# CIN tower with gathered embeddings: the first step's shifted x picked by TensorE instead of read back from DRAM

## What is computed

```
e = stack([tbl_f[ids[:, f]] for f in 39])            # (1024, 39, 16), x of the CIN
z   = einsum('bfd,bgd->bfgd', x, h)                  # h = x in layer 0
cur = relu(einsum('bfgd,fgl->bld', z, Wr) + b)       # L = 128; first half is the next h, second half goes out
out = concatenate(directs).sum(-1), then three dense layers with dense_ctx
```

## Time and profile before

| | |
|---|---|
| median of three runs | 1298.85 us |
| profiled execution | 1300.39 us, its span 1298.5 us |
| TensorE (PE) busy | 1229.6 us, 95% of the span |
| VectorE (DVE) busy | 1046.4 us, 81% |
| GpSimd (POOL) busy | 1068.2 us, 82% |
| ScalarE (ACT) busy | 750.6 us, 58% |
| mean granted TensorE clock | 0.996 |
| chain that ended last | PE 87%, POOL 4%, DVE 4%, issue 3% |

### The profile page before, as it was taken

One profiled execution on the slowest core, in us unless ns is written; L12 is line 12 of the kernel. 1 busy time (PEld: TensorE's weight loads), 2 busy tenths in 40 slices (PEclk: granted clock), 3 DMA queues, 4 the chain that ended last, 5 costly groups with the idle time before them and its releaser, 6 DMA issues.

```text
span 1298.5 us, 13246 instructions
## 1 busy us (share of the span) xinstructions
PE 1229.6 (95%) x4084; PEld 745.5 (57%) x4084; DVE 1046.4 (81%) x943; ACT 750.6 (58%) x931; POOL 1068.2 (82%) x627
## 2 busy tenths in 40 slices
PE   0379999999999999999999999999999999999999
PEld 0335555655665656655665556656656566666655
DVE  2069998888888888988888888888888888988941
ACT  1135665656555666556556656566556677777643
POOL 7528899888988898888989798888888778889942
PEclk9989999999999999999999999999999999999999
DMA  9195566655555666655556676545556665556100
GB/s 184 37 216 121 125 142 145 145 119 110 124 117 116 140 145 145 136 115 111 123 114 129 144 145 135 131 103 125 119 119 141 144 142 108 130 118 161 33 0 1
DMA packets 103424, 157.68 MB, mean 121 GB/s; under 512 B 20954, under 2 KB 33131, under 8 KB 103245
## 3 DMA queue, kind: packets, MB, share of 16 engines
q1 hardware_dynamic: 93179, 154.16, 53.5%
q0 software_dynamic: 10176, 2.70, 2.2%
HBM read 152.91 MB, written 6.19 MB: 123 GB/s over the span
## 4 chain that ended last, share of the span: by engine, by line
PE 87%; POOL 4%; DVE 4%; issue 3%; ACT 1%; DMA 1%; SPq 0%; DVEq 0%; ACTq 0%; POOLq 0%
PE curM L858 36%; PE curM L881 11%; PE curM L873 11%; PE curM L874 11%; PE curY L858 10%; POOL emb L305 3%; DVE z L566 2%; PE xk L847 2%; PE h L964 1%; PE curY L881 1%; PE curY L873 1%; PE curY L874 1%; DVE zl L619 1%; POOL zl L316 1%; ACT h L725 1%
## 5 line engine op out<-in xcount | busy, mean ns | idle before, releaser
L316 POOL TENSOR_TENSOR zl<-z,zh 128x1024 fp32r<-128x1024 f32 (+1 forms) x299 | 724.1, 2433 | 118.1 <-ACT zh L698 112.6
L566 DVE TENSOR_TENSOR z<-xr,h 128x1024 f32<-128x1024 f32 x576 | 677.4, 1216 | 154.5 <-PE curM L858 129.1
L698 ACT ACTIVATE zh<-z 128x1024 fp32r<-128x1024 f32 (+1 forms) x376 | 396.4, 1057 | 387.3 <-DVE z L566 243.4
L858 PE MATMUL curM<-z,wf 128*128 128x512 f32 (+2 forms) x1194 | 537.7, 600 | 0.0
L305 POOL DMA_INDIRECT emb<-in_tbl_dram,idx x312 | 337.6, 1082 | 100.1 <-issue 57.5
L873 PE MATMUL curM<-zh,wl 128*128 128x512 f32 (+1 forms) x642 | 340.7, 531 | 4.2 <-ACT zh L698 4.2
L858 PEld LDWEIGHTS curM<-z,wf 128*128 128x128 f32 (+2 forms) x1194 | 208.5, 188 | 195.2 <-issue 171.6
L874 PE MATMUL curM<-zh,wh 128*128 128x512 f32 (+1 forms) x642 | 251.8, 392 | 0.0
L881 PE MATMUL curM<-zl,wh 128*128 128x512 f32 (+1 forms) x642 | 200.7, 394 | 6.1 <-DVE zl L619 3.6
L873 PEld LDWEIGHTS curM<-zh,wl 128*128 128x128 f32 (+1 forms) x642 | 121.7, 190 | 72.7 <-issue 47.4
L725 ACT ACTIVATE h<-curM,bias 32x512 f32<-32x512 f32 (+1 forms) x198 | 127.9, 646 | 57.5 <-DVE z L566 51.1
(11 more groups left out here) (107 smaller groups left out, 436.9 us busy)
## 6 DMA issues: line engine op xcount, KB each, us to landing
xr<-xT SPq DMA_DIRECT2D x384, 192.0 KB
xs<-xT SPq DMA_DIRECT2D x288, 156.0 KB
xq<-xT SPq DMA_DIRECT2D x64, 256.0 KB
emb<-in_tbl_dram,idx POOLq DMA_INDIRECT x312
xs<-xT SPq DMA_DIRECT2D x64, 78.0 KB
xT<-xc SPq DMA_DIRECT2D x32, 78.0 KB
xr<-in_L_rec_W_dram SPq DMA_DIRECT2D x16, 144.0 KB
xT<-xc SPq DMA_DIRECT2D x32, 40.0 KB
```

What stands on the lines that cost most here:

```text
L316: nc.gpsimd.tensor_tensor(zl[0:n, SNUM[r, u] % NL, :], z[0:n, z_slot(r, u), :], zh[0:n, SNUM[r, u] % NH, :], ALU.subtract).then_inc(lo_poo ...
L566: return nc.vector.tensor_tensor(z[:, slot, :].rearrange("p (a n) -> p a n", a=2), x, h, ALU.mult)
L698: nc.scalar.activation(zh[0:n, SNUM[r, u] % NH, :], z[0:n, z_slot(r, u), :], ACT.Copy).then_inc(hi_ready, 1)
L858: mm = nc.tensor.matmul(cur[:, :], wf[rows, full_at(u), a, :], z[rows, z_slot(r, u), a * N:(a + 1) * N], start=start and i == 0, stop=stop ...
```

## The change

For step 0 alone, `xs` no longer comes through DRAM. VectorE lays out, from the identity matrix, a matrix `picks` of 39 x 117 for each of the seven tiles (2 + 21 small copies, ahead of its wait for `dense_turned`). TensorE multiplies `picks` by `xc` of step 0: seven float32 matmuls of 512 columns give the shifted rows in PSUM (h1 twice, curM[0], curM[1]). ScalarE copies them to `xs` in five instructions (`copy_picked`), and `product0` of step 0 waits for `x0_copied` in place of the DMAs.

SyncE loses the 11 DMAs of `load_xs(0, p)`. It now waits for `xT_written[1]` first and reads `xs` of step 1 part by part, with the write of step 2's x ahead of the last part; the waits for the weights and for `xT_written[0]` come after. `copy_xc` of step 2 moves behind the five new copies on ScalarE, and `turn` of step 2 behind the first four picks on TensorE. The matmuls without a reader go from 28 to 40, and stand ahead of the turns: they start once the first 32 gathers have landed. The count of 16 in `kind` gets the name POOL_FROM and keeps its value, and so do EARLY_FIELDS and BETWEEN, so the gathers keep their order.

```diff
+POOL_FROM = 16
-    return "D" if k == "G" and (r < 0 or (r == 0 and u < 16)) else k
+    return "D" if k == "G" and (r < 0 or (r == 0 and u < POOL_FROM)) else k
-WARM = 28
+WARM = 40
+PICKED = (1, 3, 4, 5)
+        wrapped = xr[1][0:F, 20 * L:20 * L + XR]
+        picks = xr[1][0:F, 21 * L:21 * L + T0 * R0].rearrange("p (t m) -> p t m", m=R0)
@@ sync
             write_x(1, 1)
+            sp.wait_ge(xT_written[1], 32)
+            for p in range(4):
+                sp.wait_ge(z_ready, NUM[-3, C_END + p] + 1)
+                load_xs(1, p)
+                if p == 2:
+                    sp.wait_ge(xc_copied, 3)
+                    write_x(2, 0)
             sp.wait_ge(w_hi, HI_OPS)
             sp.wait_ge(w_lo, LO_OPS)
             sp.wait_ge(w_full, FULL_OPS)
             sp.wait_ge(xT_written[0], 32)
-            for p in range(4):
-                load_xs(0, p)
-            sp.wait_ge(xc_copied, 3)
-            write_x(2, 0)
-            sp.wait_ge(xT_written[1], 32)
-            for p in range(4):
-                sp.wait_ge(z_ready, NUM[-3, C_END + p] + 1)
-                load_xs(1, p)
             for k in range(3):
                 load_xr(0, 0, k)
@@ vector
+            dve.wait_ge(ident_ready, 1)
+            nc.vector.tensor_copy(wrapped[:, 0:F], ident[0:F, 0:F]).then_inc(picks_ready, 1)
+            nc.vector.tensor_copy(wrapped[:, F:XR], ident[0:F, 0:XR - F]).then_inc(picks_ready, 1)
+            dve.wait_ge(picks_ready, 2)
+            for t in range(T0):
+                for k in range(K):
+                    nc.vector.tensor_copy(picks[:, t, k * F:(k + 1) * F],
+                                          wrapped[:, K * t + k:K * t + k + F]).then_inc(picks_ready, 1)
             dve.wait_ge(dense_turned, 1)
...
-                dve.wait_ge(xs_loaded[p], each * (s + 1) + each * LOOP * j)
+                if s == 0:
+                    dve.wait_ge(x0_copied, PICKED[p])
+                else:
+                    dve.wait_ge(xs_loaded[p], each * s + each * LOOP * j)
@@ scalar
+            def copy_picked(p, bank, a, nt, n):
+                act.wait_ge(picked, p + 1)
+                nc.scalar.activation(xs[0:n, (2 * p + a) * N:(2 * p + a + nt) * N], bank[0:n, 0:nt * N],
+                                     ACT.Copy).then_inc(x0_copied, 1)
             copy_first_emb()
-            for t in range(3):
-                copy_xc(t, 0)
+            copy_xc(0, 0)
+            copy_xc(1, 0)
+            act.wait_ge(w_lo, LO_OPS)
+            act.wait_ge(w_full, FULL_OPS)
+            copy_picked(0, h1, 0, 2, R0)
+            copy_picked(1, curM[0], 0, 1, R0)
+            copy_picked(1, curM[1], 1, 1, R0)
+            copy_picked(2, h1, 0, 2, R0)
+            copy_picked(3, curM[0], 0, 1, R0_LAST)
+            copy_xc(2, 0)
@@ tensor
+                        if u == C_END and r == -2:
+                            pe.wait_ge(x0_copied, 5)
-            pe.wait_ge(emb_copied, 1)
-            for t in range(3):
-                turn(t, 0, 0)
+            pe.wait_ge(gathered_first, 16 * FIRST_FIELDS)
             for c in range(WARM):
                 nc.tensor.matmul(h1[:, c % DQ * P:(c % DQ + 1) * P], ident[:, :], ident[:, :], start=True, stop=True)
+            def pick(t, bank):
+                n = rows0(t)
+                return nc.tensor.matmul(bank[0:n, :], picks[:, t, 0:n], xc[0][:, :], start=True, stop=True)
+            pe.wait_ge(emb_copied, 1)
+            turn(0, 0, 0)
+            turn(1, 0, 0)
+            pe.wait_ge(picks_ready, 2 + T0 * K)
             pe.wait_ge(dense_copied, 2)
+            pe.wait_ge(xc_copied, 1)
+            pick(0, h1[:, 0:N])
+            pick(1, h1[:, N:2 * N]).then_inc(picked, 1)
+            pick(2, curM[0])
+            pick(3, curM[1]).then_inc(picked, 1)
+            turn(2, 0, 0)
+            pe.wait_ge(x0_copied, 1)
+            pick(4, h1[:, 0:N])
+            pick(5, h1[:, N:2 * N]).then_inc(picked, 1)
+            pe.wait_ge(x0_copied, 2)
+            pick(6, curM[0]).then_inc(picked, 1)
```

More of the change, by code:

```diff
@@ L122 @@
 FIRST_FIELDS = 32
+GATHERED = (0, 11, 22, 32, F)
+WARM = 40
 EARLY_FIELDS, BETWEEN = 4, 29
-GATHERED = (0, 11, 22, 32, F)
-WARM = 28
+PICKED = (1, 3, 4, 5)
 def cin_tower(nc, dense, ids, tables, w_top1, b_top1, w_top2, b_top2, w_top3, w0, w1, w2, b0, b1, b2, out):
@@ L251, in cin_tower @@
         xT_written = [sem(f"xT_written{i}") for i in range(2)]
+        picks_ready = sem("picks_ready")
+        picked = sem("picked")
         x_begun = sem("x_begun")
+        x0_copied = sem("x0_copied")
         xs_loaded = [sem(f"xs_loaded{i}") for i in range(4)]
```

## The result

| | before | after |
|---|---|---|
| median | 1298.78 us (1297.95 to 1299.05, 4 runs) | 1312.36 us (1309.57 to 1314.75, 4 runs) |
| profiled execution, span | 1300.39 us, 1298.5 us | 1314.75 us, 1312.3 us |

The ratio after to before is 1.0105, 95% interval [1.008, 1.013]: 13.6 us slower, where 3.4 us faster was forecast. A second set of runs gave 1.0102 [1.0077, 1.0127].

What follows compares the result with a forecast made beforehand. TensorE, full from 150 us on, bounds the kernel, and GpSimd's start, set by SyncE, limits the gain: 4.0 us less 0.6 for the recorder's pause gives 1298.85 - 3.4 = 1295.4 us, range 1292.9 to 1298.4.

Steps and rivals of the forecast that it cites:

- The matmuls ahead of the turns: On TensorE before the turns: 80 records from 45.1 end at 56.9 us (54.7 to 58.6), costing 2.7 us.
- late warm-up rival: All 80 records at 0.21 us end at 62.0, picks at the lower clock add about 3: 1303.5 us; chance 6%.
- The compute chain: TensorE's round -3 ends at 72.7 instead of 78.05 us, at the expected full clock: gain 5.3 us.
- The picks: Step 0's float32 matmuls on TensorE: 0.93 us each; product 23 ends at 69.85, 3.0 us earlier.
- The small copies: VectorE's 23 copies at 32.5 to 37 us: no cost to gathers assumed; as rival 0.8 to 4.8 us, 7%.
- Against the median: Pause of three engines at 58 to 62 us possibly the recorder's: 0.6 us off the gain, leaving 3.4.
- SyncE's queue: SyncE's issues up to `xs` of step 2 end at 83.1 against 87.1 us: 4.0 us earlier (2.9 to 5.0).
- the only thing late at 145 us: GpSimd stays the limit (4.0 < 5.3 + 1.1); TensorE's wait for it grows from 1.1 to about 2.4 us.

Runs made afterwards that it cites:

- no_extra: The changed kernel without its 40 matmuls ahead of the turns: 1299.11 us, 1.0014 of the kernel before.
- no_extra_one_copy: The changed kernel without its 40 matmuls, its 21 small copies made by one of 819 columns: 1300.59 us, 1.0025 of the kernel before.
- one_copy_8_wide: The changed kernel with 8 matmuls of 512 columns for its 40, one copy for 21 small ones, turn 2 ahead of the picks: 1.0004 of before.
- no_extra_again: The changed kernel without its 40 matmuls, repeated unaltered in another batch: 1299.67 us, 1.0010 of the kernel before.

## Why the prediction was wrong

- **The matmuls ahead of the turns** is the step that failed. It had 80 records end at 56.9, bounds 54.7 to 58.6; they ended at 68.7. The bound allowed one pause of 1 us, though the earlier trace rows held one record of what happens: 25 of 56 records after a pause, with "issue" for a releaser. I took a rate out of two free groups and applied it to 80 records in a stretch where they come singly. Of the 17.3 us by which h came later than forecast (89.97, not 72.7), 11.8 stand ahead of the turns. The late warm-up rival had the sign, but for another reason, and 9 us short of the time.
- **The compute chain** is the other part, 5.4 us: "almost throughout busy, so full clock" failed. The granted clock was 0.50 from 76 to 84, and round -3 ended 21.2 us after the turns, where 15.8 was forecast.
- **The picks**: 0.93 us each held for the first two alone (1.94 together). The next two took 2.78, picks 4 and 5 3.76, and without matmuls ahead of them all run at the lower level. So the kernel has a choice between two losses: the matmuls that lift the clock meet the slow stretch, and without them the picks are slower than the way through DRAM (h at 77.56 against 73.57). The small copies cost the gathers next to nothing (at most one of 1.20 us in place of 0.94), as assumed.
- **Against the median** priced the pause of three engines at 58 to 62 as the recorder's. It is the kernel's own: it moves with GpSimd's chain, and times without a profile move with it. In the batch without the stretch the kernel before had a median of 1296.52 us, in the next one on the same chip 1298.06, so the pause costs the kernel before some 1.5 us in every run, not only in the recorded one. But its absence gives the picks no gain: no_extra has 1.0014 with it, no_extra_one_copy 1.0025 without it.
- **SyncE's queue** held: from the end of product 23 to GpSimd's resumption it was 13.2 us in the kernel after (85.45 to 98.69) and 13.4 in one_copy_8_wide, where the forecast had 13.5. The gain that it was to give did not come, since product 23 was late. That GpSimd would then be the only thing late at 145 us failed too: its subtraction stood so close to VectorE's that it took 2.0 us more out of it. This, and the small gain at `x_begun` (0.9 to 2.1 us), are why even the undisturbed version with eight wide matmuls is no faster than before.

Open is why some batches show no slow stretch, and what the instructions wait behind. I had thought of their fetching, on a path shared with the gathers' small packets (10,176 packets for 2.70 MB in either kernel). The DMA records speak against it: in the kernel after, one packet of kind "instruction" stands between 35 and 40 us and the next between 70 and 74, none in the stretch between them. The Trainium skill (Runtime: NRT & Kernel Launch, "Instruction fetch mechanics") has the crossing from one block of instructions to the next mostly hidden; nothing here contradicts it. Open too is why ScalarE sticks earlier once matmuls stand ahead. No version beat the kernel before by a measurable amount.

## What to carry to other kernels

An idle time that several engines show at once, with "issue" or "remote" for a releaser, is a price of that place in the program: find what else runs up to just before its end, and don't add instructions there, idle or not. Before shortening a path, look whether such a pause lies across it; then the path was not the bound. Price a new matmul at both levels of the clock, and look what TensorE did before it. When two engines are brought to nearly the same moment, ask what they share: two subtractions begun within 0.3 us of each other cost 2 us.

## What was not expected of the hardware

- While GpSimd issues gathers back to back (one per 1.25 us), all other engines may get their instructions slowly: TensorE one record per 2.80 us after 30 to 39 that ran freely, VectorE's copies of 0.18 us with idle times of 0.5 to 1.8 us between them, SyncE's issues in steps of 0.7. On TensorE it ended 3.9 to 7.7 us after the last gather, and it was absent from all four profiles of one batch among five.
- In the kernel after, TensorE was busy from 66 to 84 us without a break, and the granted clock still went from 0.98 (66 to 72) over 0.63 to 0.50 (76 to 84), so from 2.4 to 1.2 GHz, in the midst of the picks. From 57 to 66 us it had read 0.50.
- The reading can be wrong: in no_extra_again it is 1.00 from 57 to 72 us, while two picks take 3.76 us, as they do at 0.50 in the kernel after, and not 1.94.
